# Replanning the first transfers of a fused linear-attention and LoRA-expert FFN kernel

## The chip, the cores and the metric

The kernel runs on one core of one Trainium2 chip. The metric is device time in microseconds of one execution; three executions of the kernel before are known, and one more was recorded by the profiler.

## The reference, cut to what matters

```python
xn = layernorm(x)                        # x: 2 x 1024 tokens of 512 floats
Q = elu(heads(xn @ wq.T + bq)) + 1       # 16 heads of 32
K = elu(heads(xn @ wk.T + bk)) + 1
V = heads(xn @ wv.T + bv)
KV = einsum('bhsd,bhse->bhde', K, V)
att = (Q @ KV) / (Q . sum_s K + 1e-8)
att = att @ wo.T + bo
# FFN of 1376 with a router over 8 experts (top 2), shared and expert LoRA of rank 8
gate = xn @ W_gate + lora(xn) + expert_lora(xn, w)
up   = xn @ W_up   + lora(xn) + expert_lora(xn, w)
ffn  = (silu(gate) * up) @ W_down + lora + expert_lora
return x + att + ffn
```

All is float32. Each operand of a product is split into a rounded part (`_h`, made by ACT, `round_to`) and a remainder (`_l`, made by DVE, `sub`), and PE computes each product as three matmuls: high by high, high by low, low by high (`product`, L1196 to L1198).

## The kernel before

The engines are programmed each by itself, with an order written out by hand and semaphores between them. ACT is ScalarE, DVE VectorE, POOL GpSimd, PE TensorE; SP is SyncE, which here only issues transfers. The kernel has three stages: stage 1 runs over 16 tiles of 128 tokens, the attention and the FFN over groups of four tiles. The change is all in stage 1 and its preparation.

*Preparation.* SP loads x tile 0, the identity, wk (`w_raw[:, 0]`, 1 MB), x tile 1, wv (`w_raw[:, 1]`, 1 MB) and `a_raw` (the LoRA and router columns) in this order. ACT rounds wk in quarters k = 0 to 3, then wv in quarters, then a; DVE forms the remainders in the same order (`wsetl_done` counts them). DVE's layer norm of tile 0 goes through POOL (`rstd_of`) and PE's `transpose_tokens(0)`. PE meanwhile runs filler matmuls of the identity (`keep_busy`, L1264), five before these transposes and four behind them, and then the first product of wk. POOL issues five small constants (`bk`, `ebias`, `earlier`, `bq`, `zmask`) after `rstd_of(0)`.

*Stage 1 for tile t* (`stage1` in each engine's part). PE: K of tile t (`ps_k`), transposes of tile t + 1 (L1213), in even tiles `keys_by_values` of the two tiles before (L1225), V (`ps_va`, `ps_vz`), then `lora_transposed(t - 2)` (L1234), which needs DVE's `zst`. ACT: first `tokens_hi(t + 1)`, which rounds the transposed tokens into `xt[:, slot]` (L660), slot being the parity of the tile. It waits until the store of that slot's former tile, t - 1, has landed:

```python
act.wait_ge(xt_ready, t + 1)
wait(act, scr_xd[s], 16 * uses)
round_to(xt_h[:, s].rearrange("p k n -> p (k n)"), ps_xt[:]).then_inc(xth_done, 1)
```

DVE: `kb`, the routing comparison, `tokens_lo(t + 1)` (L849), then `lora_weighted(t - 2)` (`zst`), statistics and normalisation of tile t + 2, `zraw`, and at the end `lora_lo(t - 2)` (L914), after which SP may store z of tile t - 2. Tiles 2 to 7 are a loop of pairs on ACT, DVE and PE; tiles 8 to 15 are written out (there ACT and DVE also split wq, at tiles 8 to 11, and wo, at 12 to 15).

*SP in stage 1.* For tile t it loads x of tile t + 3 (L391) and stores the split tokens to `scr_x` (L425). It then stores z of tile t - 2 (L415), in even tiles of the loop loads `x3a` back from `scr_x` (L405), and loads a chunk of `dn` (L442). All its transfers run on one queue. Its loop covers tiles 2 to 9 in four passes, tiles 10 to 15 are written out. In the loop it stores z of tile 2p behind the stage1 of tile 2p + 2. Behind the stage1 of tile 0 it issues eight constants of later stages (L431 to L433: `hmask`, `hcol`, `hrow_raw`, `lomask`, `bdn_raw` 512 KB, `sb_dn` 256 KB, `bv_b`, `bo_b`, a broadcast of one row of 2 KB to all 128 partitions), then the whole of wo and wq (L435, L436) into the two halves of `w_raw`, which are free once `wsetl_done` has reached 8.

## Time and profile before

| what | us |
|---|---|
| median of 3 runs (lowest, highest) | 675.92 (674.55, 676.27) |
| the profiled execution, its own time | 675.29 |
| its span | 673.5 |
| PE busy | 661.8 (98%) |
| DVE, ACT, POOL busy | 375.6, 256.3, 126.9 |

Times in the profile are microseconds from the start of the span. "Idle before <-releaser" is the engine's own wait and what ended it. A matmul's duration is modelled and overlaps the next; the distance between starts is the pace. `bank` stands for any PSUM bank. L660 and L849 are the helpers for rounding and remainder, so the name of the tile tells what is meant. The profile's granted clock reads 1.00 throughout; PE's two speeds in the first microseconds are seen only in the pitch of its products.

### The profile page before, as it was taken

To read this page: it belongs to the slowest core of one execution; us is meant where nothing else is said; L and a number is where in the kernel's file an instruction comes from. 1 tells how busy PE (TensorE), PEld (TensorE's weight loads), DVE (VectorE), ACT (ScalarE), POOL (GpSimd) and SP (SyncE) were. 2 spreads that over 40 slices of the span, in tenths; PEclk is the share of its full clock that TensorE was granted. 3 is DMA by queue.
4 is the path that set the end of the run, shared out by engine and by line. 5 is a ranking of instruction groups with operands and counts; after the bars stand their busy time and mean duration, and the time that the engine had idled before them with its cause. 6 is when DMAs were issued, how large, how long until landed. Compare 5 with 4: busy or idle time off the path is not lost.

```text
span 673.5 us, 10336 instructions
## 1 busy us (share of the span) xinstructions
PE 661.8 (98%) x3568; PEld 544.2 (81%) x3568; DVE 375.6 (56%) x696; ACT 256.3 (38%) x412; POOL 126.9 (19%) x290
## 2 busy tenths in 40 slices
PE   7999999999999999999999999999999999999998
PEld 6889899977677788888888888888888888888886
DVE  5577788778775966344346433445444336534433
ACT  4343445467235324323233332333233314323321
POOL 3456666635256130000000000000000000000000
PEclk9999999999999999999999999999999999999999
DMA  7946566753853679940024100012400002300001
GB/s 222 328 158 225 194 202 203 249 213 150 307 218 115 253 242 3 43 161 0 0 79 169 82 0 0 0 63 78 187 0 0 0 0 78 126 0 0 0 0 62
DMA packets 40634, 74.21 MB, mean 110 GB/s; under 512 B 19280, under 2 KB 19920, under 8 KB 38688
## 3 DMA queue, kind: packets, MB, share of 16 engines
q1 hardware_dynamic: 40400, 73.56, 37.5%
q0 software_dynamic: 208, 0.30, 0.4%
q8 instruction: 16, 0.26, 0.2%
q14 instruction: 10, 0.08, 0.0%
HBM read 52.81 MB, written 21.04 MB: 110 GB/s over the span
## 4 chain that ended last, share of the span: by engine, by line
PE 89%; DVE 4%; issue 2%; ACT 1%; POOL 1%; DMA 1%; SPq 0%; POOLq 0%; DVEq 0%; ACTq 0%
PE bank L1196 20%; PE bank L1197 19%; PE bank L1198 19%; PE bank L1438 18%; PE bank L1411 6%; PE bank L1424 2%; DVE den L1049 1%; PE bank L1422 1%; DMA w_raw<-in_wkT 1%; PE bank L1213 1%; PE bank L1225 1%; PE bank L1311 1%; DVE qf_odd L1007 1%; PE bank L1449 1%; PE bank L1451 1%
## 5 line engine op out<-in xcount | busy, mean ns | idle before, releaser
L1196 PE MATMUL bank<-x,up_h 128*128 128x512 f32 (+1 forms) x352 | 137.1, 390 | 0.2 <-DVE x3r L1014 0.2
L1197 PE MATMUL bank<-x,up_h 128*128 128x512 f32 (+1 forms) x352 | 137.2, 390 | 0.0
L1198 PE MATMUL bank<-x,up_l 128*128 128x512 f32 (+1 forms) x352 | 137.1, 390 | 0.0
L1139 DVE TENSOR_TENSOR hf<-bank,silu 128x512 f32<-128x512 f32 x44 | 30.4, 691 | 155.4 <-issue 135.6
L1438 PE MATMUL bank<-dn,hid_h 128*128 128x512 f32 x352 | 108.7, 390 | 0.0
L660 ACT ACTIVATE hid_h<-hf 128x512 fp32r<-128x512 f32 x44 | 27.8, 632 | 142.4 <-DVE hf L1139 142.4
L1196 PEld LDWEIGHTS bank<-x,up_h 128*128 128x128 f32 x352 | 66.1, 188 | 16.5 <-issue 0.7
L1438 PEld LDWEIGHTS bank<-dn,hid_h 128*128 128x128 f32 x352 | 65.9, 188 | 14.7 <-DVE res L1158 0.6
L1197 PEld LDWEIGHTS bank<-x,up_h 128*128 128x128 f32 x352 | 66.1, 188 | 14.2
L1198 PEld LDWEIGHTS bank<-x,up_l 128*128 128x128 f32 x352 | 66.1, 188 | 13.8
L849 DVE TENSOR_TENSOR up_l<-up_raw,up_h 128x1024 fp32r<-128x1024 f32 x44 | 55.0, 1249 | 26.9 <-ACT up_h L660 26.9
L1438 PE MATMUL bank<-dn,hid_l 128*128 128x512 f32 x176 | 68.5, 389 | 0.0
L660 ACT ACTIVATE up_h<-up_raw 128x1536 fp32r (+1 forms) x44 | 64.5, 1473 | 1.7 <-DVE qf_odd L1007 1.7
L809 ACT ACTIVATE silu<-bank 128x512 f32<-128x512 f32 x44 | 26.3, 599 | 101.0 <-PE bank L1411 101.0
L1411 PE MATMUL bank<-z,up_h 128*128 128x512 f32 x176 | 54.2, 389 | 0.0
L849 DVE TENSOR_TENSOR hid_l<-hf,hid_h 128x512 fp32r<-128x512 f32 x44 | 30.5, 692 | 35.5 <-ACT hid_h L660 35.5
L660 ACT ACTIVATE dn<-dn_raw 128x576 fp32r (+1 forms) x44 | 30.1, 683 | 33.5 <-PE bank L1424 22.6
L1196 PE MATMUL bank<-va_h,xt 128*128 128x384 f32 (+1 forms) x128 | 41.5, 324 | 0.0
L1197 PE MATMUL bank<-va_l,xt 128*128 128x384 f32 (+1 forms) x128 | 40.3, 315 | 0.0
L1198 PE MATMUL bank<-va_h,xt 128*128 128x384 f32 (+1 forms) x128 | 40.3, 315 | 0.0
L849 DVE TENSOR_TENSOR up_h<-up_raw,up_h 64x256 fp32r<-64x256 f32 x88 | 38.6, 439 | 0.6
L1438 PEld LDWEIGHTS bank<-dn,hid_l 128*128 128x128 f32 x176 | 33.0, 188 | 7.0
(165 smaller groups left out, 1081.7 us busy)
## 6 DMA issues: line engine op xcount, KB each, us to landing
x<-scr_x SPq DMA_DIRECT2D x7, 2048.0 KB, 9.3
up_raw<-in_ffn_up SPq DMA_DIRECT2D x11, 768.0 KB, 7.9
scr_x<-xt SPq DMA_DIRECT2D x16, 512.0 KB, 5.3
xin<-in_x SPq DMA_DIRECT2D x16, 256.0 KB, 4.6
scr_z<-zt SPq DMA_DIRECT2D x16, 256.0 KB, 2.0
x3r<-in_x SPq DMA_DIRECT2D x16, 256.0 KB, 3.5
scr_att<-x3r SPq DMA_DIRECT2D x16, 256.0 KB, 2.7
z<-scr_z SPq DMA_DIRECT2D x4, 1024.0 KB, 4.9
```

Of the source, the lines that this page charges most:

```text
L660: return nc.scalar.activation(dst, src, ACT.Copy)
L809: nc.scalar.activation(silu[:], ps_g[:], ACT.Silu).then_inc(silu_done, 1)
L849: return nc.vector.tensor_tensor(dst, a, b.bitcast(F32), ALU.subtract)
L1007: nc.vector.tensor_tensor(qf[g % 2][:, c, :], qf[g % 2][:, c, :], qexp[:, c % 2, :], ALU.add).then_inc(q_done, 1)
L1049: nc.vector.reciprocal(den[:], den[:]).then_inc(rden_done, 1)
L1139: nc.vector.tensor_tensor(hf[:], ps_u[:], silu[:], ALU.mult).then_inc(h_done, 1)
L1196: nc.tensor.matmul(dst, lh, rh, start=start, stop=False, **kw)
L1197: nc.tensor.matmul(dst, lh, rl, start=False, stop=False, **kw)
L1198: return nc.tensor.matmul(dst, ll, rh, start=False, stop=stop, **kw)
L1411: last = nc.tensor.matmul(dst[:], up_h[:, s, col:col + P], z4[:, :, a * 2 + b, :], start=False, stop=(b == 1))
L1424: return nc.tensor.matmul(ps_zd[0:ER, :], dn_h[:, s, DNB - 1], hid_l[:, s, :], start=False, stop=last, skip_group_check=True)
L1438: d = nc.tensor.matmul(ps_out[j][:], h[:, s, cols], w[:, s, 0:DNB - 1], start=(first and i == 0), stop=False, skip_group_check=True)
```

## The change

- wk is loaded in quarters with a semaphore each: 1 and 3 by SP, 0 and 2 by ACT (its own queue). wv is loaded in four quarters by SP. ACT rounds tile 0's tokens after quarter 1, not 0; DVE likewise forms their remainder after quarter 1. DVE takes the statistics of tile 1 after the first quarter of wv, and normalises it after the third.
- a is split in two halves on ACT and DVE; PE waits for the second at its k = 2 of the first tile (`upper`).
- POOL issues `bk` once wk's last quarter has landed, and the other four constants after `rstd_of(1)`. DVE waits for `bk` alone before the tiles, and for the other four behind `zraw` of tile 0, where it also makes `nbq`.
- SP issues one quarter of wq and one of wo at the head of each of its four loop passes. The eight constants go behind the z store of tile 8, in tile 10 (`load_constants`).
- ACT waits for `wq_in` and `wo_in` at the splits; ACT and DVE wait for `s2_in` where the constants are first read.

```diff
-STAGE2_LOADS = 10
+STAGE2_LOADS = 8
...
             load_x(0, 0)
             sp.dma_start(ident[:], dram["ident"]).then_inc(ident_in, 16)
-            sp.dma_start(w_raw[:, 0], dram["wkT"]).then_inc(wk_in, 16)
+            for k in range(1, KD, 2):
+                sp.dma_start(w_raw[:, 0, k], dram["wkT"][:, k]).then_inc(wk_in[k], 16)
             load_x(1, 1)
-            sp.dma_start(w_raw[:, 1], dram["wvT"]).then_inc(wv_in, 16)
+            for k in range(KD):
+                sp.dma_start(w_raw[:, 1, k], dram["wvT"][:, k]).then_inc(wv_in[k], 16)
...
             stage1(0, 0)
-            for dst, name in ((hmask, "headmask"), (hcol, "headcol"), (hrow_raw, "headrow"), (lomask, "lomask"), (bdn_raw, "b_dn"), (sb_dn, "sb_dn")):
-                sp.dma_start(dst[:], dram[name]).then_inc(s2_in, 16)
-            sp.dma_start(bv_b[:], dram["bv"]).then_inc(s2_in, 16)
-            sp.dma_start(bo_b[:], dram["bo"].to_broadcast([P, D])).then_inc(s2_in, 16)
+            stage1(1, 1)
+
+            def load_constants():
+                for dst, name in ((hmask, "headmask"), (hcol, "headcol"), (bv_b, "bv"), (hrow_raw, "headrow"),
+                                  (lomask, "lomask"), (bdn_raw, "b_dn"), (sb_dn, "sb_dn")):
+                    sp.dma_start(dst[:], dram[name]).then_inc(s2_in, 16)
+                sp.dma_start(bo_b[:], dram["bo"].to_broadcast([P, D])).then_inc(s2_in, 16)
+
             sp.wait_ge(wsetl_done, 2 * KD)
-            sp.dma_start(w_raw[:, 0], dram["woT"]).then_inc(s2_in, 16)
-            sp.dma_start(w_raw[:, 1], dram["wqT"]).then_inc(s2_in, 16)
...
-            stage1(1, 1)
-            with sp.Fori(0, GT) as p:
+            with sp.Fori(0, KD) as p:
+                sp.dma_start(w_raw[:, 1, bass.ds(p, 1)], dram["wqT"][:, bass.ds(p, 1)]).then_inc(wq_in, 16)
+                sp.dma_start(w_raw[:, 0, bass.ds(p, 1)], dram["woT"][:, bass.ds(p, 1)]).then_inc(wo_in, 16)
                 stage1(2 * p + 2, 0)
...
                 if t < TILES - 1:
                     store_z(t - 2)
+                if t == 2 * GT + 2:
+                    load_constants()
                 if t < FC:
                     load_dn(t - 2)
...
             rstd_of(0)
-
-            for dst, name in ((bk_b, "bk"), (eb_b, "ebias")):
-                pool.dma_start(dst[:], dram[name].to_broadcast([P, dst.shape[1]])).then_inc(consts_in, 16)
+            pool.wait_ge(wk_in[KD - 1], 16)
+            pool.dma_start(bk_b[:], dram["bk"].to_broadcast([P, D])).then_inc(bk_in, 16)
+            pool.wait_ge(wv_in[1], 16)
+            rstd_of(1)
+            pool.dma_start(eb_b[:], dram["ebias"].to_broadcast([P, E])).then_inc(consts_in, 16)
...
-            rstd_of(1)
             rstd_of(2)
...
+            act.wait_ge(vare_done, 1)
+            for k in range(0, KD, 2):
+                act.dma_start(w_raw[:, 0, k], dram["wkT"][:, k]).then_inc(wk_in[k], 16)
             act.sem_inc(scr_zd, 16)
-            act.wait_ge(wk_in, 16)
             for k in range(KD):
+                act.wait_ge(wk_in[k], 16)
                 round_to(wk_h[:, k], w_raw[:, 0, k]).then_inc(wseth_done, 1)
-                if k == 0:
+                if k == 1:
                     tokens_hi(0, 0, 0)
-            act.wait_ge(wv_in, 16)
             for k in range(KD):
+                act.wait_ge(wv_in[k], 16)
                 round_to(wv_h[:, k], w_raw[:, 1, k]).then_inc(wseth_done, 1)
             act.wait_ge(a_in, 16)
-            round_to(a_h, a_raw[:]).then_inc(wseth_done, 1)
+            for k in range(0, KD, 2):
+                round_to(a_h[:, k:k + 2], a_raw[:, k:k + 2]).then_inc(wseth_done, 1)
...
                 nc.vector.tensor_copy(zraw[:, s], ps_z).then_inc(zraw_done, 1)
+                if first:
+                    dve.wait_ge(consts_in, 64)
+                    nc.vector.tensor_scalar(nbq[:], bq_c[:], -1.0, None, ALU.mult).then_inc(nbq_done, 1)
...
-                if k == 0:
+                if k == 1:
                     tokens_lo(0, 0)
-            stats_of(1, 1, 0)
             for k in range(KD):
                 dve.wait_ge(wseth_done, KD + k + 1)
                 sub(wv_l[:, k], w_raw[:, 1, k], wv_h[:, k]).then_inc(wsetl_done, 1)
-                if k == 1:
+                if k == 0:
+                    stats_of(1, 1, 0)
+                if k == 2:
                     normalise(1, 1)
```

The order of SP's transfers around tiles 10 and 11, where the scr_x store that ACT waits for at tile 12 stands. Before:

```order
L391 DMA xin<-in_x 128x512
L425 DMA scr_x<-xt 128x1024
L415 DMA scr_z<-zt 128x512
L442 DMA dn_raw<-in_ffn_dn 128x576
L391 DMA xin<-in_x 128x512
L425 DMA scr_x<-xt 128x1024
```

The same place in the change (`bdn_raw` and `sb_dn_sb` are constants of the down projection):

```order
L394 DMA xin<-in_x 128x512
L430 DMA scr_x<-xt 128x1024
L420 DMA scr_z<-zt 128x512
L439 DMA hmask<-in_headmask 128x4
L439 DMA hcol<-in_headcol 128x128
L439 DMA bv_b<-in_bv 128x128
L439 DMA hrow_raw<-in_headrow 128x128
L439 DMA lomask_sb<-in_lomask 128x1
L439 DMA bdn_raw<-in_b_dn 128x1024
L439 DMA sb_dn_sb<-in_sb_dn 128x512
L440 DMA bo_b<-in_bo 128x512
L448 DMA dn_raw<-in_ffn_dn 128x576
```

The eight constants now stand between the z store of tile 8 and the load of `dn`, ahead of x of tile 14 and the scr_x store of tile 11.

DVE's queue before the first `kb` (tile 0), before the change:

```order
L849 TENSOR_TENSOR wk_l<-w_raw,wk_h 128x512
L849 TENSOR_TENSOR xt<-bank,xt 128x512
L849 TENSOR_TENSOR wk_l<-w_raw,wk_h 128x512 x3
L853 BN_STATS stats<-xin 128x6
L856 MEMSET spare 128x1
L857 BN_AGGR mv<-stats 128x2
L849 TENSOR_TENSOR va_l<-w_raw,va_h 128x512 x2
L862 TENSOR_SCALAR xn<-xin,mv,rstd 128x512
```

and in the change:

```order
L865 TENSOR_TENSOR wk_l<-w_raw,wk_h 128x512 x2
L865 TENSOR_TENSOR xt<-bank,xt 128x512
L865 TENSOR_TENSOR wk_l<-w_raw,wk_h 128x512 x2
L865 TENSOR_TENSOR va_l<-w_raw,va_h 128x512
L869 BN_STATS stats<-xin 128x6
L872 MEMSET spare 128x1
L873 BN_AGGR mv<-stats 128x2
L865 TENSOR_TENSOR va_l<-w_raw,va_h 128x512 x2
L878 TENSOR_SCALAR xn<-xin,mv,rstd 128x512
```

The remainder of tile 0's tokens (`xt`) moves behind the second quarter of wk; the statistics of tile 1 move behind the first quarter of wv.

## Rows read from the trace of the kernel before

**Rows 1.** The page, part 1: busy time, share of the span and instructions.

```profile
PE 661.8 (98%) x3568; PEld 544.2 (81%) x3568; DVE 375.6 (56%) x696; ACT 256.3 (38%) x412; POOL 126.9 (19%) x290
```

**Rows 2.** TensorE's waits over the whole run: total, times, longest (us).

```profile
PE bank L1234 <- DVE zst L904: 1.3, 1, 1.3
PE bank L1196 <- DVE xt L849: 1.2, 1, 1.2
```

**Rows 3.** Chain of waits, first 18 us: start us, us, what.

```profile
1.67 6.38 DMA w_raw<-in_wkT
...
10.09 0.79 PE bank L1196
10.89 0.43 PE bank L1197
...
13.69 0.23 PE bank L1198
```

**Rows 4.** Timeline, first 10 us: start us, us, engine, line, work, [idle before <-releaser].

```profile
3.77 2.50 PE L1264 MATMUL bank<-ident_sb 128*128 128x128 f32 x10 [3.77 <-DMA ident_sb<-in_ident]
...
7.01 1.91 PE L1264 MATMUL bank<-ident_sb 128*128 128x128 f32 x8
...
9.35 0.68 DVE L849 TENSOR_TENSOR xt<-bank,xt 128x512 fp32r<-128x512 f32 x1
```

**Rows 5.** Timeline of PE, 28 to 107 us: L1225 and L1234.

```profile
28.85 0.77 PE L1225 MATMUL bank<-vf,kf 128*32 128x33 f32 x64
...
34.80 0.44 PE L1234 MATMUL bank<-ident_sb,zst 128*128 128x128 f32 x2 [1.34 <-DVE zst L904]
...
46.26 0.77 PE L1225 MATMUL bank<-vf,kf 128*32 128x33 f32 x64
...
61.35 0.77 PE L1225 MATMUL bank<-vf,kf 128*32 128x33 f32 x64
...
72.90 0.38 PE L1234 MATMUL bank<-ident_sb,zst 128*128 128x128 f32 x2
...
106.59 0.78 PE L1225 MATMUL bank<-vf,kf 128*32 128x33 f32 x64
```

**Rows 6.** Timeline of ACT: the roundings of tokens.

```profile
33.06 0.60 ACT L660 ACTIVATE xt<-bank 128x512 fp32r<-128x512 f32 x1 [5.86 <-DMA scr_x<-xt]
...
63.06 0.60 ACT L660 ACTIVATE xt<-bank 128x512 fp32r<-128x512 f32 x1 [2.06 <-DMA scr_x<-xt]
...
69.53 0.60 ACT L660 ACTIVATE xt<-bank 128x512 fp32r<-128x512 f32 x1 [0.80 <-PE bank L1213]
```

**Rows 7.** Timeline of SP: DMA issues, start us, us of issuing.

```profile
15.46 0.43 SPq L431 DMA_DIRECT2D hmask<-in_headmask  x1
...
19.44 0.43 SPq L433 DMA_DIRECT2D bo_b<-in_bo  x1
...
21.57 0.46 SPq L425 DMA_DIRECT2D scr_x<-xt  x1
...
54.72 0.35 SPq L415 DMA_DIRECT2D scr_z<-zt  x1
...
62.13 0.35 SPq L415 DMA_DIRECT2D scr_z<-zt  x1
...
69.92 0.35 SPq L415 DMA_DIRECT2D scr_z<-zt  x1
...
99.77 0.34 SPq L415 DMA_DIRECT2D scr_z<-zt  x1
...
101.13 0.43 SPq L425 DMA_DIRECT2D scr_x<-xt  x1
```

**Rows 8.** DMA issues at 21.5 and 101.1 us: KB, us to landing.

```profile
scr_x<-xt SPq DMA_DIRECT2D x1, 512.0 KB, 11.5
...
scr_x<-xt SPq DMA_DIRECT2D x1, 512.0 KB, 4.7
```

**Rows 9.** DMA issues of the first 45 us: KB, us to landing.

```profile
bo_b<-in_bo SPq DMA_DIRECT2D x1, 256.0 KB, 6.0
```

More of the change, by code:

```diff
@@ L249, in program @@
         consts_in = sem("consts_in")
+        bk_in = sem("bk_in")
         ident_in = sem("ident_in")
-        wk_in = sem("wk_in")
-        wv_in = sem("wv_in")
+        wk_in = [sem(f"wk_in{k}") for k in range(KD)]
+        wv_in = [sem(f"wv_in{k}") for k in range(KD)]
         a_in = sem("a_in")
@@ L292, in program @@
         s2_in = sem("s2_in")
+        wq_in = sem("wq_in")
+        wo_in = sem("wo_in")
         nbq_done = sem("nbq_done")
@@ L685, in stage1 @@
                 if isinstance(t, int) and t in WQ_PART:
-                    act.wait_ge(s2_in, 16 * STAGE2_LOADS)
+                    act.wait_ge(wq_in, 16 * KD)
                     round_to(wq_h[:, WQ_PART[t]], w_raw[:, 1, WQ_PART[t]]).then_inc(wqh_done, 1)
                 if isinstance(t, int) and t in WO_PART:
+                    act.wait_ge(wo_in, 16 * KD)
                     round_to(wo_h[:, WO_PART[t]], w_raw[:, 0, WO_PART[t]]).then_inc(woh_done, 1)
@@ L768, in _ @@
             act.wait_ge(kf_done, TILES)
+            act.wait_ge(s2_in, 16 * STAGE2_LOADS)
             round_to(hrow[:], hrow_raw[:]).then_inc(hrow_done, 1)
@@ L969, in _ @@
                 sub(wv_l[:, k], w_raw[:, 1, k], wv_h[:, k]).then_inc(wsetl_done, 1)
-                if k == 1:
+                if k == 0:
+                    stats_of(1, 1, 0)
+                if k == 2:
                     normalise(1, 1)
-            dve.wait_ge(wseth_done, 2 * KD + 1)
-            sub(a_l, a_raw[:], a_h).then_inc(wsetl_done, 1)
+            for k in range(0, KD, 2):
+                dve.wait_ge(wseth_done, 2 * KD + k // 2 + 1)
+                sub(a_l[:, k:k + 2], a_raw[:, k:k + 2], a_h[:, k:k + 2]).then_inc(wsetl_done, 1)
             dve.sem_inc(kvacc_done, 1)
-            dve.wait_ge(consts_in, 80)
+            dve.wait_ge(bk_in, 16)
             def heads_of(b):
+                dve.wait_ge(s2_in, 16 * STAGE2_LOADS)
                 for c in range(KD):
@@ L984, in heads_of @@
                                         hmask[:].unsqueeze(1).unsqueeze(3).to_broadcast([P, KD, HC, DK]), ALU.mult).then_inc(kvm_done, 1)
-            nc.vector.tensor_scalar(nbq[:], bq_c[:], -1.0, None, ALU.mult).then_inc(nbq_done, 1)
             tiles(dve, stage1)
@@ L1198, in product, with tile_of @@
                 return nc.tensor.matmul(dst, ll, rh, start=False, stop=stop, **kw)
-            def tile_of(dst, s, wh, wl, split_before=None):
+            def tile_of(dst, s, wh, wl, split_before=None, upper=None):
                 for k in range(KD):
@@ L1204, in tile_of @@
                         pe.wait_ge(wsetl_done, split_before + k + 1)
+                    if upper is not None and k == 2:
+                        pe.wait_ge(wsetl_done, upper)
                     last = product(dst, (xt_h[:, s, k, :], xt_l[:, s, k, :]), (wh[:, k, :], wl[:, k, :]),
@@ L1254, in stage1 @@
                     pe.wait_ge(wsetl_done, 2 * KD + 1)
-                tile_of(ps_vz, s, va_h[:, :, VA:], va_l[:, :, VA:]).then_inc(vz_ready, 1)
+                tile_of(ps_vz, s, va_h[:, :, VA:], va_l[:, :, VA:], upper=2 * KD + 2 if first else None
+                        ).then_inc(vz_ready, 1)
                 if behind(t, 2):
```

## Prediction

> **What bounds the kernel now.** I read the page first, then TensorE's waits, then the chain of waits and the timelines at the places the change touches. TensorE (PE) is busy 661.8 us of the span [rows 1]: nothing counts but what stops it or slows its matmuls. The list of its waits [rows 2] holds two that this change can reach. One is 1.2 us before the first product. The other is 1.3 us before the transposes of L1234, near 34 us.
>
> The start: the chain of waits [rows 3] runs through the load of wkT (1 MB, landed at 8.05), its first rounding on ACT, the first remainders on DVE, and reaches PE at 10.09. PE had run filler matmuls of L1264 and four transposes from 3.77 up to 8.92 (7.01 + 1.91) [rows 4]. From 10.89 the products of L1196 to L1198 come every 0.43 us, from 13.69 on every 0.23 us [rows 3]. The first pitch belongs to the 1.2 GHz level of PE's clock, the second to 2.4 GHz. The clock rose about 3.3 us after the products had begun.
>
> The stall near 34: PE's `keys_by_values` (L1225) starts once per pair of tiles; from 46.26 to 61.35 is 15.09 us, an undisturbed pair. From 28.85 to 46.26 is 17.41 [rows 5], so the disturbed pair lost 2.3 us. ACT rounded the tokens of tile 3 at 33.06 after 5.86 us of waiting for a store of scr_x [rows 6]. That store (tile 1's, slot 1) was issued at 21.57 [rows 7] and landed 11.5 us later [rows 8]. Ahead of it in the SP queue were eight constants, all of wo and wq and an x tile.
>
> **The change part by part.**
>
> *Start.* wk comes in quarters, so ACT's first two roundings need 512 KB, not 1 MB. Before, the 1 MB (behind x tile 0 and ident) took 6.4 us from its issue [rows 3]; half of it I estimate to be there 1.5 to 2.5 us sooner, by 5.6 to 6.6. Two roundings, each of the tokens' size (0.60) [rows 6], end by 7.9 at the latest, then the tokens' own rounding (0.60) and remainder (0.68) [rows 4] by 9.2. PE is held by its own filler until 8.92 anyway. So the first product moves from 10.09 to about 9.0: **-1.1 us**. The bounds are 0 (quarters no faster than the whole) and -2.0. The second is reached if the clock also rises sooner: eight products ran at the slow pitch [rows 3], and the 0.2 us they lose each cannot all be had, since DVE's remainders of wv and a (8 operations of about 0.68 and two small ones between 9.0 and 15) then hold PE. The splits of a in halves, the later POOL constants (eb, earlier, bq, zmask) and the negation of bq moved behind tile 0 I cost at nothing. What covers them is that PE needs what follows on DVE, tile 2's tokens, only some 5 us later. If the POOL constants land late, up to 1 us of DVE waiting hides there.
>
> *The stall near 34.* Constants, wo and wq no longer lie ahead of tile 1's store; only one quarter of each is issued, behind it. **-2.3 us** [rows 5]. What is late next is the ordinary pair time, so the whole of it comes back.
>
> *wq and wo by quarters.* Each of four loop passes issues two more transfers (512 KB) on SP, ahead of the even tile's x load and store. The odd tile's store already has a 512 KB transfer (x3a) ahead of it, and it shows what that does. From the store of z at 54.72 [rows 7] to ACT's tokens at 63.06 [rows 6], which waited for the landing, is 8.34 us. PE did not stall in that pair [rows 5]. By this pattern the even tile's tokens come at 62.13 + 8.34 + some 0.3 of issue = 70.8 in place of 69.53 [rows 6, 7]. From tokens to L1234 took 1.74 us (33.06 to 34.80) [rows 5, 6], so 72.5, and PE reaches L1234 at 72.90 [rows 5]: 0.4 us of slack. The lag feeds back, as the next z store hangs on these tokens. I take **+0.2 us**; bounds 0 and +2.6 (a rival, below).
>
> *The constants at tile 10.* They do not vanish, they move into SP's queue between the z store of tile 8 (99.77) and the scr_x store of tile 11 (101.13) [rows 7]. ACT's rounding of tile 13's tokens waits for that store, exactly as tile 3's waited for tile 1's. Before, the burst took from 15.46 to the end of bo's issue at 19.87, 4.4 us [rows 7], so the store is issued at 105.5. Bounds for its landing T. Lowest: only the issue is late and it lands 4.7 us on [rows 8], or less if an issue costs 0.43 throughout: 109.4 to 110.3. Highest: bo landed 6.0 us after 19.44 [rows 9], at 25.4, so 10.0 us after the burst began. In the new place that is 110.1, with dn, x and the store (1.06 MB) behind it. The 2.75 MB behind bo before (wo, wq, x, scr_x) took from 25.4 to 33.07, 360 GB/s, so 2.9 us more: 113.0. I take 112.0, nearest to the upper end, because the same eight transfers and the same broadcast are in front of the same store. The loss: before, tokens at 33.06 were 4.21 us behind L1225 at 28.85 and cost 2.33 us [rows 5, 6]. Here L1225 is at 106.59 [rows 5]. The loss is 2.33 + (T - 106.59 - 4.21) = T - 108.5: **+3.5 us**, bounds +0.9 and +4.5.
>
> The Trainium skill ("DMA: Bandwidth & Descriptors", Specifications) puts the fabric's ceiling at 435 GB/s. By it alone the 2.08 MB from bdn to the store, issued from about 102.9, would be in by some 109.7 (an estimate with its 2 us of fixed cost), and this term would be +1.2. The rows speak against it: bo, 256 KB, took 6.0 us to land [rows 9], where a store of twice its size took 4.7 [rows 8].
>
> *Their readers.* ACT's, DVE's and POOL's new waits on s2_in come at tile 14 and later, 25 us behind the loads: nothing. The same holds for wq_in at tile 8, where ACT needs the last quarter several us after its issue.
>
> **The sum.** -1.1 - 2.3 + 0.2 + 3.5 = +0.3 us, against the profiled execution's own 675.29 us (its span is 673.5). That is 675.6. The profiled run lies 0.6 us under the median of the three, 675.92; they spread over 1.7 us, more than most single terms here. About 0.3% (2.0 us) is what a measurement of this kernel can tell from no change: below 673.9 counts as faster, above 677.9 as slower.
>
> **Rivals.**
>
> 1. *The burst at tile 10 is cheap* (the lower bound: T near 109.4 to 110.3, +0.9 to +1.8). For it: in the new place no 2 MB of weights follows. Against it: the same broadcast. It gives 675.29 - 1.1 - 2.3 + 0.2 + 0.9 to 1.8 = 673.0 to 673.9. Chance 0.22.
> 2. *The clock rises sooner.* Closing the 1.2 us gap leaves PE busy from the first filler on. For it: the clock rose 3.3 us after the products began, and with no gap the filler may count too. Against it: 5 us of filler and transposes did not raise it before. It takes 0.9 us more off: 674.7, or 672.1 to 673.0 with rival 1. Chance 0.10, half of that below 673.9. The Trainium skill ("TensorE: Matmul & The Clock Gate", Part 4) says transposes do not count as busy for the clock; the four transposes lie between the two batches of filler, and the trace agrees so far as the clock stayed low across them.
> 3. *The stores become the loop's bound*: slower. Place: SP's queue at the head of each pass. The landing of the even tile's store is followed 6.9 us later by the next odd z store (63.06 to 69.92 for the other parity [rows 6, 7]), which starts the next store. With 8.34 us from z to landing that loop takes 15.2 us against PE's 15.09, so it would be level, with the slack above to spare. From about 0.4 us of added landing time on it decides. If the 512 KB add 1.3 us, three passes lose 1.3 each, less some 1.3 of slack: +2.6 in place of +0.2, 678.0. Chance 0.10.
> 4. *The start does not do what it says*: the quarters, in 2 KB rows, land as late as the whole did. Then 675.29 - 2.3 + 0.2 + 3.5 = 676.7. Chance 0.08. The Trainium skill ("DMA: Bandwidth & Descriptors", Issuing engines are not separate DMA queues) says that a second issuing engine saves only issue time.
>
> The forecast itself has 0.50, from 673.8 to 677.2. Faster: 0.22 + 0.05 + 0.05 of the forecast's edge = 0.32. Slower: 0.10. Same: 0.58. The range, 672.4 to 677.7, leaves out rival 3 and the lowest corner of rivals 1 and 2.
>
> **What would show it.** The first product at 8.9 to 9.3, the clock's rise at 12.3 to 13.4. No wait of ACT for scr_x near 33, and 15.1 us from the first L1225 to the second. A wait of ACT for scr_x of 4 us or more at tile 12, with PE idle before L1234 some 111 us into the old time scale. Even-tile tokens waiting on scr_x in the loop. I am wrong if that pair stays at 15.1 us, or if the pairs of the loop grow.

## The result, and the profile after

| | before | the change |
|---|---|---|
| median of 5 runs (lowest, highest), us | 674.94 (674.55, 676.27) | 679.88 (678.98, 681.89) |
| ratio (95% interval) | | 1.0073 (1.0060 to 1.0086) |
| profiled execution, its own time; span | 675.29; 673.5 | 679.69; 677.9 |
| PE busy | 661.8 | 662.6 |

The change is 4.9 us slower, outside the range of 672.4 to 677.7. PE does the same work in the same time; the loss is in its waits. TensorE's waits in the profile after (total, times, longest, in us), the three that the change touched:

```profile
PE bank L1257 <- DVE zst L920: 5.0, 2, 3.2
...
PE bank L1217 <- DVE va_l L865: 0.8, 1, 0.8
PE bank L1217 <- DVE xt L865: 0.6, 1, 0.6
```

The wait of 1.2 us at the start became 0.6 and 0.8. The one of 1.3 us for `zst` [rows 2] became two, 5.0 us together. (Lines have shifted: L1225 is now L1248, L1234 is L1257, L1196 to L1198 are L1217 to L1219, L1213 is L1236.) PE's timeline after, `keys_by_values` once per pair of tiles, and each stop behind the start:

```profile
28.16 0.77 PE L1248 MATMUL bank<-vf,kf 128*32 128x33 f32 x64
43.26 0.77 PE L1248 MATMUL bank<-vf,kf 128*32 128x33 f32 x64
58.57 0.77 PE L1248 MATMUL bank<-vf,kf 128*32 128x33 f32 x64
74.02 0.77 PE L1248 MATMUL bank<-vf,kf 128*32 128x33 f32 x64
87.47 0.44 PE L1257 MATMUL bank<-ident_sb,zst 128*128 128x128 f32 x2 [1.75 <-DVE zst L920]
91.06 0.77 PE L1248 MATMUL bank<-vf,kf 128*32 128x33 f32 x64
106.14 0.77 PE L1248 MATMUL bank<-vf,kf 128*32 128x33 f32 x64
113.98 0.44 PE L1257 MATMUL bank<-ident_sb,zst 128*128 128x128 f32 x2 [3.24 <-DVE zst L920]
126.24 0.77 PE L1248 MATMUL bank<-vf,kf 128*32 128x33 f32 x64
140.88 0.77 PE L1248 MATMUL bank<-vf,kf 128*32 128x33 f32 x64
```

The starts of the same line before that [rows 5] does not hold, from PE's timeline of the kernel before:

```profile
76.43 0.77 PE L1225 MATMUL bank<-vf,kf 128*32 128x33 f32 x64
...
121.70 0.77 PE L1225 MATMUL bank<-vf,kf 128*32 128x33 f32 x64
...
136.35 0.76 PE L1225 MATMUL bank<-vf,kf 128*32 128x33 f32 x64
```

Subtracting start from start gives the whole account, in us:

| stretch | before | after | difference |
|---|---|---|---|
| up to the first start | 28.85 | 28.16 | -0.7 |
| first pair (the stall near 34) | 17.41 | 15.10 | -2.3 |
| two pairs of the loop | 30.17 | 30.76 | +0.6 |
| pair with tiles 8 and 9 | 15.08 | 17.04 | +2.0 |
| pair with tiles 10 and 11 | 15.08 | 15.08 | 0 |
| pair with tiles 12 and 13 (the stop behind the burst) | 15.11 | 20.10 | +5.0 |
| next pair | 14.65 | 14.64 | 0 |
| sum | | | +4.5 (spans: +4.4) |

**The start.** PE's timeline after, first products of wk, the wait in V of tile 0, K of tile 1:

```profile
9.48 0.51 PE L1217 MATMUL bank<-wk_h,xt 128*128 128x512 f32 x1 [0.61 <-DVE xt L865]
9.82 0.39 PE L1218 MATMUL bank<-wk_l,xt 128*128 128x512 f32 x1
10.06 0.39 PE L1219 MATMUL bank<-wk_h,xt 128*128 128x512 f32 x1
...
15.20 0.44 PE L1217 MATMUL bank<-va_h,xt 128*128 128x384 f32 x1 [0.82 <-DVE va_l L865]
...
17.84 0.50 PE L1217 MATMUL bank<-wk_h,xt 128*128 128x512 f32 x1
```

Products come every 0.23 us from 9.82 on, the pitch of 2.4 GHz that the kernel before reached near 13.4 [rows 3]. So the clock rose about 3.5 us sooner, yet K of tile 1 starts only 0.7 us sooner (17.84 against 18.57): V of tile 0 has to wait for DVE's remainders. PE was no longer what bound this stretch. These are single executions, and the sooner rise is not shown to come from the change: a run with the old start ("The kernel before, its whole block one store later", below) has the fast pitch from its second product too.

**Tile 8 and the burst.** ACT's timeline after: tokens of an even tile in the loop, the first rounding of wq (tile 8), the tokens of tile 10, the tokens of tile 13:

```profile
68.54 0.60 ACT L670 ACTIVATE xt<-bank 128x512 fp32r<-128x512 f32 x1 [2.71 <-DMA scr_x<-xt]
...
82.50 0.63 ACT L670 ACTIVATE wq_h<-w_raw 128x512 fp32r<-128x512 f32 x1 [4.25 <-DMA w_raw<-in_wqT]
...
85.17 0.60 ACT L670 ACTIVATE xt<-bank 128x512 fp32r<-128x512 f32 x1 [1.25 <-DMA scr_x<-xt]
...
112.25 0.60 ACT L670 ACTIVATE xt<-bank 128x512 fp32r<-128x512 f32 x1 [5.91 <-DMA scr_x<-xt]
```

DVE's remainder of that quarter of wq:

```profile
83.24 0.69 DVE L865 TENSOR_TENSOR wq_l<-w_raw,wq_h 128x512 fp32r<-128x512 f32 x1 [2.23 <-ACT wq_h L670]
```

The issues of SP's queue that these wait for (the last quarter of wq, the first and last constant, the scr_x store of tile 11):

```profile
77.48 0.36 SPq L451 DMA_DIRECT2D w_raw<-in_wqT  x1
...
100.31 0.43 SPq L439 DMA_DIRECT2D hmask<-in_headmask  x1
...
103.65 0.43 SPq L440 DMA_DIRECT2D bo_b<-in_bo  x1
...
105.08 0.43 SPq L430 DMA_DIRECT2D scr_x<-xt  x1
```

ACT at tile 8 waits until all four quarters of wq are there, and the fourth is issued only in the pass that brings tile 8's own store. The wait reaches PE through DVE, which stands 2.23 us for the rounding and then has a full queue up to `zst`. A second wait ends at nearly the same time: the tokens of tile 10 came at 85.17, released by the landing of tile 8's scr_x store. PE's stop (87.47, in tile 9) has both behind it; it is called the stop at tile 8 below. At tile 12 the store is issued 4.0 us later than before (105.08, not 101.13) and lands 7.1 us on, not 4.7 [rows 7, 8].

**The clock behind the long stop.** Windows of the profile after: stretch, then length, busy time of PE, PEld, DVE, ACT, POOL, then PEclk, DMA share, GB/s:

```profile
110.70:113.98 3.28, 0.04 (x1) 0.00 (x1) 1.11 (x5) 1.70 (x4) 0.00 (x0) 1.00 1.04 399
...
115.30:118.70 3.40, 3.40 (x10) 2.54 (x9) 2.60 (x7) 0.90 (x4) 2.76 (x9) 0.50 0.05 19
```

Shortly behind the idle time of 3.24 us the granted clock is 0.50 (1.2 GHz) for 3.4 us. By these figures, 3.4 us at half speed, the fall cost some 1.7 us (an estimate). The first window shows also that the 16 DMA engines were full (share 1.04, 399 GB/s) while PE stood.

### The profile page after: what moved, and what is told of

Read it like the earlier page. It is cut to its first block, busy times and chain, and to the rows that moved or that the text cites. A ratio compares the mean times of both kernels' runs of the same rounds, so it can differ in the third digit from the quotient of the medians.

```text
span 677.9 us, 10370 instructions
## 1 busy us (share of the span) xinstructions
PE 662.6 (98%) x3568; PEld 544.0 (80%) x3568; DVE 375.9 (55%) x697; ACT 256.4 (38%) x413; POOL 126.7 (19%) x290
## 4 chain that ended last, share of the span: by engine, by line
PE 78%; POOL 6%; issue 5%; DVE 5%; DMA 3%; ACT 2%; SPq 1%; POOLq 1%; ACTq 0%; DVEq 0%
PE bank L1462 17%; PE bank L1217 16%; PE bank L1218 16%; PE bank L1219 16%; PE bank L1435 6%; PE bank L1448 2%; DVE den L1070 1%; PE bank L1446 1%; DMA scr_x<-xt 1%; DMA w_raw<-in_wkT 1%; POOL vare L580 1%; POOL rstd L582 1%; DMA w_raw<-in_wqT 1%; POOL gt L607 1%; PE bank L1335 1%
## 5 line engine op out<-in xcount | busy, mean ns | idle before, releaser
L1217 PE MATMUL bank<-x,up_h 128*128 128x512 f32 (+1 forms) x352 | 137.1, 390 | 0.2 <-DVE x3r L1035 0.2
L1219 PE MATMUL bank<-x,up_l 128*128 128x512 f32 (+1 forms) x352 | 137.1, 389 | 0.0
L1217 PEld LDWEIGHTS bank<-x,up_h 128*128 128x128 f32 x352 | 66.1, 188 | 16.5 <-issue 0.7
L1219 PEld LDWEIGHTS bank<-x,up_l 128*128 128x128 f32 x352 | 66.1, 188 | 13.8
L1217 PE MATMUL bank<-va_h,xt 128*128 128x384 f32 (+1 forms) x128 | 41.9, 327 | 0.8 <-DVE va_l L865 0.8
L1219 PE MATMUL bank<-va_h,xt 128*128 128x384 f32 (+1 forms) x128 | 40.3, 315 | 0.0
```

The source lines that it names most:

```text
L1217: nc.tensor.matmul(dst, lh, rh, start=start, stop=False, **kw)
L1219: return nc.tensor.matmul(dst, ll, rh, start=False, stop=stop, **kw)
```

## The experiments

All line numbers within one kernel differ by one or two from those above where its edit adds or removes lines. Each batch is set against its own runs of the kernel before: 674.72 in the first (four kernels), 675.22 in the second (four), 674.84 in the third (four).

### ACT waits for each quarter alone

```diff
-                    act.wait_ge(wq_in, 16 * KD)
+                    act.wait_ge(wq_in, 16 * (WQ_PART[t] + 1))
```

> The change, with ACT waiting at tiles 8 to 11 for one more quarter of wq each time, not for all four at tile 8. Theory 1 (each loss has its own place: 2.0 us by ACT's wait of 4.25 us for wq at tile 8, 5.0 at tiles 12 and 13 by the burst of constants, 0.6 in the loop): the wait for wq is gone, the pair that took 17.0 us takes about 15.3, and the kernel is 1.7 to 2.0 us faster than the change (about 678). Theory 2 (the loop's stores have become the bound, and the stop at tile 8 is only where their lag comes due): ACT's tokens stay late, PE stops at the same place for scr_x, and under 0.7 us is gained.

Measured: 679.38 us, 1.0074 (1.0059 to 1.0089). PE's timeline, the stops at tile 8 and tile 12:

```profile
86.18 0.44 PE L1257 MATMUL bank<-ident_sb,zst 128*128 128x128 f32 x2 [0.94 <-DVE zst L920]
...
113.54 0.69 PE L1257 MATMUL bank<-ident_sb,zst 128*128 128x128 f32 x2 [4.07 <-DVE zst L920]
```

ACT's timeline, the tokens of tile 10:

```profile
84.44 0.60 ACT L670 ACTIVATE xt<-bank 128x512 fp32r<-128x512 f32 x1 [3.41 <-DMA scr_x<-xt]
```

The stop at tile 8 is halved, and PE reaches the pair of tile 12 1.3 us sooner (104.86, not 106.14). Then it stands 0.8 us longer, and in the profiles 0.5 us is left (spans of 677.4 and 677.9). In time it is not resolved: the ratios to the kernel before are 1.0074 here and 1.0073 in the change. The burst was issued 1.5 us sooner (98.81) too, but ACT's tokens came at 111.81, 0.4 us sooner. Here the gain ahead of a stop that transfers end was mostly lost in it. Why this store took longer behind its own issue (8.2 us from 103.60 to the tokens, against 7.2) no row settles. 0.9 us of stop is left at tile 8 and it is not wq's: the even tile's tokens (84.44) waited 3.41 us for a scr_x store there. The wait for wq is gone as theory 1 had it, but the gain is that of theory 2.

### Constants back to the beginning, the rest as in the change

```diff
             stage1(0, 0)
-            stage1(1, 1)
-
             def load_constants():
...
+            load_constants()
+            stage1(1, 1)
...
-                if t == 2 * GT + 2:
-                    load_constants()
```

> The change, with the eight constants back behind the store of tile 0; wq and wo stay by quarters in the loop. Theory 1: the stop of 3.2 us at tile 12 and the slow matmuls behind it go (pair 15.1 in place of 20.1), and near 34 us nothing comes back, since constants alone leave tile 1's store landing near 27: 5 us faster than the change, about 675. Theory 2 (the burst only pays once wherever it stands): some 2.3 us come back near 34, and the gain is about 2.7.

Measured: 674.23 us, 0.9989 (0.9980 to 0.9998), 5.7 us under the change, as theory 1 had it. This one edit takes the whole loss back. The pair of tile 12 is 15.1 us again, and the first pair stays at 15.1: at the beginning the constants cost nothing once the 2 MB of wo and wq no longer follow. (Its profiled execution, 677.19, is the slowest of its 12: the stop at tile 8 was 2.21 us there, and the clock fell behind it.)

### The kernel before, its whole block one store later

The eight constants, wo and wq are issued behind `stage1(1, 1)` instead of ahead of it.

```diff
-            for dst, name in ((hmask, "headmask"), (hcol, "headcol"), ...
-            sp.dma_start(w_raw[:, 1], dram["wqT"]).then_inc(s2_in, 16)
...
             stage1(1, 1)
+            for dst, name in ((hmask, "headmask"), (hcol, "headcol"), ...
+            sp.dma_start(w_raw[:, 1], dram["wqT"]).then_inc(s2_in, 16)
             with sp.Fori(0, GT) as p:
```

> The kernel before, with the block of eight constants, wo and wq issued behind tile 1's store of scr_x, not ahead of it; nothing else. Theory 1 (what stops PE near 34 us is only that tile 1's store stands behind the block): ACT's wait of 5.9 us for scr_x goes, the pair of 17.4 us falls to 15.1 to 15.6 (tile 2's store, now behind the block, lands near 35, when it is just wanted), 1.8 to 2.3 us faster than before. Theory 2 (the bytes must be paid wherever they stand): the wait moves to tile 4's tokens and 0 to 0.5 us is gained.

Measured: 675.19 us, 1.0017 (1.0000 to 1.0033). PE's timeline:

```profile
9.27 0.50 PE L1195 MATMUL bank<-wk_h,xt 128*128 128x512 f32 x1 [1.32 <-DVE xt L848]
9.61 0.39 PE L1196 MATMUL bank<-wk_l,xt 128*128 128x512 f32 x1
...
28.25 0.77 PE L1224 MATMUL bank<-vf,kf 128*32 128x33 f32 x64
...
41.47 0.44 PE L1233 MATMUL bank<-ident_sb,zst 128*128 128x128 f32 x2 [1.51 <-DVE zst L903]
```

The stall near 34 is gone and stands at 41.5, on the next store of scr_x, with 1.51 us (1.34 before [rows 5]). 3.2 MB in one block has to be paid somewhere (theory 2): to move it is worth nothing, to spread it is (the runs with quarters, below). The first lines show something else. The start here is the old one, yet the first product comes at 9.27, the products behind it at 0.23 us each, and the first `keys_by_values` at 28.25, 0.6 us sooner than in the profile before and 0.1 later than in the change. With the new start that line stood at 26.98 to 30.42 in the profiled executions. So one pair of profiles does not price the start.

### The start alone

wk and wv in quarters as in the change, constants and the whole of wo and wq as before.

```diff
             stage1(0, 0)
-            stage1(1, 1)
...
+            load_constants()
+
             sp.wait_ge(wsetl_done, 2 * KD)
+            sp.dma_start(w_raw[:, 0], dram["woT"]).then_inc(wo_in, 16)
+            sp.dma_start(w_raw[:, 1], dram["wqT"]).then_inc(wq_in, 16)
+            stage1(1, 1)
...
             with sp.Fori(0, KD) as p:
-                sp.dma_start(w_raw[:, 1, bass.ds(p, 1)], dram["wqT"][:, bass.ds(p, 1)]).then_inc(wq_in, 16)
-                sp.dma_start(w_raw[:, 0, bass.ds(p, 1)], dram["woT"][:, bass.ds(p, 1)]).then_inc(wo_in, 16)
```

> The start of the change alone (quarters of wk and wv on two queues, a in halves, POOL's constants later), with the constants and the whole of wo and wq where the kernel before had them. Theory 1: first product near 9.5, K of tile 1 some 0.7 us sooner than before, the stall near 34 as before, and no stops at tiles 8 and 12: 0.7 us faster than before, up to 2 in a run where the clock rises sooner. Theory 2 (the start gives nothing in the runs' mean, as the clock's rise differs from run to run): within 0.3 us of before.

Measured: 675.48 us, 1.0006 (0.9997 to 1.0016). PE's timeline, and the window behind the stop (columns as above):

```profile
27.54 0.77 PE L1248 MATMUL bank<-vf,kf 128*32 128x33 f32 x64
...
34.82 0.44 PE L1257 MATMUL bank<-ident_sb,zst 128*128 128x128 f32 x2 [2.67 <-DVE zst L920]
```

```profile
36.00:39.20 3.20, 3.20 (x9) 2.46 (x9) 1.64 (x6) 0.90 (x4) 2.56 (x9) 0.50 0.00 0
```

PE arrives 1.3 us sooner than before (27.54, not 28.85) and goes on at the same moment, 34.82 against 34.80 [rows 5]: the store's landing sets it. The stop is 1.3 us longer, and behind it the clock fell, as it did not behind the shorter one. That holds for this execution: in eight of the twelve the mean granted clock was 1.000, in four 0.997, which is one such fall. While the stall stands, the start's gain is nothing (675.48 against 674.72).

### All three mended

Constants early, a wait per quarter, and the quarters of each pass behind the even tile's store.

```diff
...
             with sp.Fori(0, KD) as p:
+                stage1(2 * p + 2, 0)
                 sp.dma_start(w_raw[:, 1, bass.ds(p, 1)], dram["wqT"][:, bass.ds(p, 1)]).then_inc(wq_in, 16)
                 sp.dma_start(w_raw[:, 0, bass.ds(p, 1)], dram["woT"][:, bass.ds(p, 1)]).then_inc(wo_in, 16)
-                stage1(2 * p + 2, 0)
...
-                    act.wait_ge(wq_in, 16 * KD)
+                    act.wait_ge(wq_in, 16 * (WQ_PART[t] + 1))
```

> The change with three mends: the constants back behind tile 0's store, ACT waiting for one quarter of wq at a time, and the loop's quarters of wq and wo issued behind the even tile's store of scr_x, not ahead of it. Theory 1 (the extra bytes ahead of the stores that ACT waits for are the cause of all three stops, and there is idle time of the queue behind the even store): no stop before L1257 anywhere, all pairs at 15.1 us, no fall of the clock; 671.5 to 672.5, some 2.5 us faster than before and 7 to 8 faster than the change. Theory 2 (the store chain needs more than PE's 15.1 us per pair as soon as wq and wo are in the loop): pairs of 15.3 to 15.5 and a stop near tile 8 stay, 674 or more.

Measured: 671.94 us, 0.9952 (0.9940 to 0.9963): 3.3 us faster than the kernel before, some 8 us faster than the change. PE's timeline:

```profile
8.54 0.75 PE L1216 MATMUL bank<-wk_h,xt 128*128 128x512 f32 x1
...
26.98 0.77 PE L1247 MATMUL bank<-vf,kf 128*32 128x33 f32 x64
...
117.47 0.77 PE L1247 MATMUL bank<-vf,kf 128*32 128x33 f32 x64
```

Six pairs in 90.49 us, 15.08 each, and no wait for `zst`. The waits that share one semaphore are sound only because each quarter lands (some 5 us) long before the next is issued (15 us): the Trainium skill ("DMA: Bandwidth & Descriptors", Why a DMA increments its semaphore by 16 and not by 1) warns that with two transfers in flight on one semaphore the count can pass before the first is there. A semaphore for each quarter would be the form to keep.

### Is it bo's broadcast?

Only `bo` goes back to the beginning, seven constants stay at tile 10.

```diff
             stage1(0, 0)
+            sp.dma_start(bo_b[:], dram["bo"].to_broadcast([P, D])).then_inc(s2_in, 16)
             stage1(1, 1)
...
-                sp.dma_start(bo_b[:], dram["bo"].to_broadcast([P, D])).then_inc(s2_in, 16)
```

> The change, with one of the eight constants, the broadcast bo (256 KB), back behind tile 0's store; seven constants (0.96 MB) stay in tile 10. Theory 1 (bo's broadcast is the slow part of the burst, 2 to 2.5 us of it): tile 11's store lands 2.5 to 3 us sooner, PE's stop falls from 3.2 to about 0.7 us and the clock does not fall; 4 us faster than the change, about 676. Theory 2 (a byte is a byte; bo is a fifth of the burst): the stop falls by 0.5 (issue) to 1.1 us, to over 2 us; the clock still falls or not, 679 to 677.5.

Measured: 678.02 us, 1.0047 (1.0032 to 1.0062), 1.9 us under the change. PE's timeline:

```profile
112.91 0.44 PE L1257 MATMUL bank<-ident_sb,zst 128*128 128x128 f32 x2 [2.41 <-DVE zst L920]
```

The stop is 0.8 us shorter, ACT's tokens come at 111.17, 1.1 us sooner. An issue (0.48 us) and 256 KB at the 400 GB/s of the stretch (0.66 us) are 1.1 us. So bo weighs what its issue and its bytes weigh (theory 2); the other seven carry the rest. In this profile the clock did not fall, and the pair took 18.03 us (105.87 to 123.90), 2.1 less than in the change. But in four of the six executions the mean granted clock was 0.997, as in the change, so the clock is not shown to be the remainder of the 1.9 us, and no run here tells what is.

### The burst behind the store that is next

In tile 10 the constants go ahead of `store_z(8)`, directly behind the tile's own scr_x store, where SP's queue would be idle.

```diff
                 stage1(t, t % 2, more=(t + 3 < TILES))
+                if t == 2 * GT + 2:
+                    load_constants()
                 if t < TILES - 1:
                     store_z(t - 2)
-                if t == 2 * GT + 2:
-                    load_constants()
```

> The change, with the same burst of eight constants in tile 10, but issued behind tile 10's store of scr_x and ahead of the z store of tile 8 (SP waits there some 5 us for z with an empty queue). Theory 1 (what costs is that the burst delays tile 11's store): the burst is issued and mostly landed before z comes, tile 11's store lands near its old time or up to 1 us later, the stop at tile 12 goes; 4.5 to 5 us faster than the change, about 675. Theory 2 (the bytes must be paid in any place of that tile): the stop stays above 2 us.

Measured: 675.37 us, 0.9998 (0.9986 to 1.0009), 4.5 us under the change. PE's timeline:

```profile
111.25 0.44 PE L1257 MATMUL bank<-ident_sb,zst 128*128 128x128 f32 x2 [0.54 <-DVE zst L920]
```

SP's timeline, the first constant:

```profile
96.03 0.43 SPq L439 DMA_DIRECT2D hmask<-in_headmask  x1
```

The same bytes, in the same tile, two statements up in the code: of the 3.24 us of stop 0.54 are left, since the burst now starts at 96.03, some 4 us sooner, and the queue has gone through most of it when the next store comes. What cost the change its 5 us was the place in the queue, not the transfers.

### How much of it is the clock

Filler matmuls of the identity ahead of tile 12's `lora_transposed` keep PE at work through the stop: 24 in one kernel, 14 in the other.

```diff
+                if isinstance(t, int) and t == 12:
+                    keep_busy(ps_t, FILL)
                 if behind(t, 2):
                     lora_transposed(t - 2)
```

> The change, with 24 filler matmuls of the identity (as keep_busy has them) on PE at tile 12, ahead of L1257, in the 3.2 us in which PE stood idle; the results of the filler are used by nothing. It measures what the fall of the clock costs. Theory 1 (the idle time let the clock fall to 1.2 GHz for 3.4 us, from 115.3 to 118.7): the stop stays, the clock does not fall, tile 13's pace is undisturbed: 1.3 to 1.6 us faster than the change. Theory 2 (the slow stretch behind the stop has another cause): no gain, or 0.3 us lost where the filler is longer than the stop.

> e8 with 14 filler matmuls in place of 24. The 24 took 5.4 us, 2.0 us more than the stop, and still the next L1249 came only 0.3 us later than in the change: with the clock kept up, 1.6 us were won and 2.0 lost. Fourteen take 3.1 us and fit into the stop. Theory 1 (the fall of the clock costs 1.6 us): 1.3 to 1.7 us faster than the change, 678.2 to 678.6. Theory 2 (the clock's fall is worth nothing, the filler's end is hidden otherwise): as slow as the change, 679.9.

Measured: 679.96 us, 1.0076 (1.0055 to 1.0096) with 24, and 679.33 us, 1.0062 (1.0044 to 1.0079) with 14. PE's timelines, first with 24, then with 14:

```profile
110.55 5.52 PE L1291 MATMUL bank<-ident_sb 128*128 128x128 f32 x48
115.90 0.38 PE L1258 MATMUL bank<-ident_sb,zst 128*128 128x128 f32 x2
...
126.52 0.77 PE L1249 MATMUL bank<-vf,kf 128*32 128x33 f32 x64
```

```profile
110.21 3.29 PE L1291 MATMUL bank<-ident_sb 128*128 128x128 f32 x28
113.42 0.44 PE L1258 MATMUL bank<-ident_sb,zst 128*128 128x128 f32 x2
...
124.42 0.77 PE L1249 MATMUL bank<-vf,kf 128*32 128x33 f32 x64
```

In neither profile did the clock fall behind the filler. From the transposes to the next `keys_by_values` took 10.62 us with 24 and 11.00 with 14, against 12.26 in the change (113.98 to 126.24): the fall cost that stretch 1.3 to 1.6 us. 24 were too many: they ended 1.7 us behind the time that `zst` needs (tokens at 112.46, and 1.73 us from tokens to transposes, as in the change). The 14 ended just in time (111.69 and 113.42). With 14 the pair took 18.66 us, 1.4 less than the change, but the medians differ by 0.5 us only, in different batches, and their intervals overlap. With 14 the clock stayed up in every execution: the mean granted clock was 0.999 or 1.000 in all six, and 0.994 or 0.997 in all five of the change. The kernel before hints at a price in time: its executions at 0.997 had medians 1.1, 0.5 and 1.5 us above those at 1.000 in the three batches, which goes along with a fall but does not prove it the cause. So the clock's part is shown in the profiles, in the time it is not resolved.

### The kernel before with quarters in the loop

The old start, constants at the old place, quarters behind the even tile's store, with a wait for each quarter of wq.

```diff
-            sp.dma_start(w_raw[:, 0], dram["woT"]).then_inc(s2_in, 16)
-            sp.dma_start(w_raw[:, 1], dram["wqT"]).then_inc(s2_in, 16)
...
                 stage1(2 * p + 2, 0)
+                sp.dma_start(w_raw[:, 1, bass.ds(p, 1)], dram["wqT"][:, bass.ds(p, 1)]).then_inc(wq_in, 16)
+                sp.dma_start(w_raw[:, 0, bass.ds(p, 1)], dram["woT"][:, bass.ds(p, 1)]).then_inc(wo_in, 16)
```

> The kernel before with only the transfers of wq and wo changed: by quarters in the loop behind the even store (as in e5), the constants where they were, the start as it was. Beside e5 (671.9) it prices the start where no stall near 34 stands in its way. Theory 1 (e4 gained nothing from the start because the stall near 34 ends at a time set by the transfers, and ate it): this kernel is 2.3 us faster than before, 672.9, and e5 is 1.0 us faster than it. Theory 2 (the start gives nothing anywhere): as fast as e5 within 0.4 us, and 3.3 us faster than before.

Measured: 672.90 us, 0.9973 (0.9962 to 0.9984): 1.9 us under the kernel before, all pairs 15.1 us, no wait for `zst`. The stall's removal alone is worth this. The mended kernel with the new start lies 1.0 us below it (671.94; by the ratios, since the batches differ, 1.4, with intervals that just touch): that is what the start is worth when no stall takes it back.

### The two mends of the loop, each taken away

The mended kernel with the quarters at the head of the pass again, as in the change:

```diff
             with sp.Fori(0, KD) as p:
-                stage1(2 * p + 2, 0)
                 sp.dma_start(w_raw[:, 1, bass.ds(p, 1)], dram["wqT"][:, bass.ds(p, 1)]).then_inc(wq_in, 16)
                 sp.dma_start(w_raw[:, 0, bass.ds(p, 1)], dram["woT"][:, bass.ds(p, 1)]).then_inc(wo_in, 16)
+                stage1(2 * p + 2, 0)
```

> e5 with the loop's quarters of wq and wo again at the head of each pass, ahead of the even store; constants early and one-quarter waits stay. It prices the place of the quarters alone. Theory 1 (the even store is delayed by their 512 KB; the lag feeds back through z): pairs of 15.1 to 15.4 and a stop of about 0.9 us at tile 8 as in e1; 1 to 1.5 us slower than e5. Theory 2 (the place does not matter once the waits for all quarters are gone): within 0.3 us of e5.

Measured: 674.07 us, 0.9976 (0.9964 to 0.9988). And the mended kernel with the wait for all four quarters:

```diff
-                    act.wait_ge(wq_in, 16 * (WQ_PART[t] + 1))
+                    act.wait_ge(wq_in, 16 * KD)
```

> e5 with ACT's wait at tile 8 for all four quarters of wq again, the quarters behind the even store. The last quarter is then issued about 1.7 us later than in the change. Theory 1 (that wait stops ACT, and through it the tokens): ACT waits 5 us or more for wq, PE stops 2 to 3 us at tile 8; 2.5 to 4 us slower than e5. Theory 2 (it is the lag of the stores, not the wait): 0 to 1 us slower than e5.

Measured: 673.47 us, 0.9974 (0.9963 to 0.9984). PE's timelines, the stop at tile 8 in the first and in the second, then ACT's in the second:

```profile
89.16 0.44 PE L1256 MATMUL bank<-ident_sb,zst 128*128 128x128 f32 x2 [1.77 <-DVE zst L919]
```

```profile
86.06 0.44 PE L1256 MATMUL bank<-ident_sb,zst 128*128 128x128 f32 x2 [1.32 <-DVE zst L919]
```

```profile
81.09 0.63 ACT L669 ACTIVATE wq_h<-w_raw 128x512 fp32r<-128x512 f32 x1 [4.46 <-DMA w_raw<-in_wqT]
```

Each alone brings back a stop at tile 8 and 1.5 to 2.1 us by the medians (by the ratios, since the batches differ, 1.6 for the place of the quarters and 1.5 for the wait). The kernel that lacks both mends (constants early, above) is 2.3 us above the mended one, 2.5 by the ratios, less than the two prices together. They are two causes of one stop, so their prices do not add. To mend one of the two gains 0.2 to 1.0 us (from medians to ratios), to mend both gains 2.3 to 2.5.

## Why the prediction was wrong

**The frame held.** PE's work did not change, its waits and clock made the whole difference, and the pairs of `keys_by_values` accounted for all of it. What failed is the sum of the terms.

**The start, -1.1: measured -0.7.** The first product came at 9.48, not 9.0: ACT's part ended at 8.50 as reckoned, but DVE had two remainders of wk in front of the tokens':

```profile
7.53 1.29 DVE L865 TENSOR_TENSOR wk_l<-w_raw,wk_h 128x512 fp32r<-128x512 f32 x2 [1.53 <-ACT wk_h L670]
8.74 0.68 DVE L865 TENSOR_TENSOR xt<-bank,xt 128x512 fp32r<-128x512 f32 x1
```

The prediction's sum left these two out (the lines are from DVE's timeline after). Rival 2's clock did rise sooner, and bought little for the reason given there: DVE's remainders held PE (the wait of 0.82 us at 15.20). But the sooner rise came in a run with the old start as well, and the -0.7 lies within what the first `keys_by_values` varies by from one profiled execution to the next, so it is luck as much as a measure. In time, with no stall behind it, the start is worth 1.0 to 1.4 us, as forecast. The prediction did not see that such a gain is lost when a stop that transfers end comes behind it; the start alone measured nothing.

**The stall near 34, -2.3: right.** 17.41 became 15.10.

**wq and wo by quarters, +0.2: measured +0.6 in the loop, and a share of the stop at tile 8.** The mechanism was as told: from the z store (59.54) to the even tile's tokens (68.54) took 9.0 us, where the prediction had 8.34 + 0.3, and 0.4 us of slack were all there was. Over the profiled executions with quarters ahead of the store those two pairs took 30.2 to 30.8 us in place of 30.17, so they lost up to 0.6 us. The rest of the lag came due at tile 8: in the mended kernel with the quarters ahead again, and a wait for each quarter alone, the two pairs lost nothing and the pair of tile 8 took 17.07 us, 2.0 more, with a stop of 1.77. In time the place of the quarters costs 1.6 to 2.1 us. This was rival 3's mechanism, at 0.6 to 0.8 of its price of 2.6; the term of 0.2 was too small by 1.4 to 1.9.

**"Their readers: nothing" was the other step that failed: the rest of the +2.0 at tile 8.** The prediction had ACT need the last quarter several us behind its issue. It did not read the wait's number: at tile 8 ACT needs one quarter but waits for four, and the fourth, issued at 77.48, landed 5 us later. The rounding came at 82.50 after 4.25 us, DVE's remainder behind it, and so `zst` was late. With the quarters behind the store and only this wait wrong, the stop is 1.32 us and the kernel 1.5 us slower. The lag of the stores stood at the same place, so to mend this wait alone let PE pass tile 8 1.3 us sooner in the profile and gave nothing that the time resolves (1.0074 against 1.0073).

**The constants at tile 10, +3.5: measured +5.0.** T was right: 112.25, where the prediction said 112.0. The burst put the store's issue 4.0 us later, not 4.4. Of the 1.5 us missing, 0.25 is T, and 0.45 is PE, which arrived sooner (106.14, not 106.59) at a stop whose end does not move. The last 0.8 lies behind the stop: the pair lost 1.8 us more than its stop of 3.24, where the prediction's scale (2.3 us lost on a stop of 1.3) had 1.0. The runs with filler put the clock's fall at 1.3 to 1.6 us of these 1.8. The prediction carried the loss behind a short stop over to a long one, and across that length the clock level changed. "The same broadcast" as the reason for T fell: bo weighs its bytes. So that T came out near 112.0 is in part luck.

**The rivals.** The cheap burst did not occur. For the slower side the prediction had one rival, the stores in the loop. Its lag was one of the two causes of the stop at tile 8, the wait for all quarters was in no rival, and the burst's upper bound, 4.5 us, had no room for the clock. With +2.0 and +5.0 in place of 0 and +3.5 the sum is +3.8; with the loop and the start as measured it is +4.6, the account up to rounding.

**The steps that failed** are thus three: the quarters' term (+0.2; alone it measured 1.6 to 2.1), the readers' term (0; alone it measured 1.5, the two together 2.3 to 2.5), and the loss at tile 12 (+3.5; it measured 5.0, the clock's fall behind the long stop being what the sum did not have).

**What the cause is,** by the runs: beside PE's 15.1 us per pair there is a second bound, nearly level with it, the circle z store, scr_x store, landing, ACT's tokens, DVE's `zst`, next z store (the circle is read from the order of the queues; what the rows show is that a scr_x store's landing ends the stops near 34, at 41.5 and at tile 12, and one of the two waits at tile 8). What SP's one queue issued ahead of a scr_x store lengthened it, and the same burst issued where the queue had time to spare cost next to nothing. The change took 3.2 MB out from ahead of one such store, put 1.2 MB ahead of another, and half a MB ahead of each even tile's in the loop.

## What to carry to other kernels

In a queue like SP's here, a transfer's place relative to the store that an engine waits for decides its price: put loads that nobody needs soon directly behind that store, in small pieces, not ahead of it. Check each wait's number against the issue time of the last transfer it counts, not against the first. Here a gain ahead of a stop that a transfer ends was worth nothing until the stop was gone, so the stop comes first. Price a term by the kernels' times with and without it: one profile each cannot tell 0.7 us at the start from the spread.

## What the runs showed of the hardware

- PE's clock fell to the lower level for about 3.4 us after idle times of 2.21, 2.67, 3.24 and 4.07 us, and after one of only 1.90 us ahead of the first product (the kernel before with quarters in the loop: 8.04 to 9.94, granted clock 0.50 from 10.5 to 13.5). It did not after 2.41 us (bo early), 2.07 us (24 filler matmuls) and 1.90 us (14 filler matmuls, both at tile 8). So between 1.9 and 2.4 us the stop's length alone does not decide. The Trainium skill ("TensorE: Matmul & The Clock Gate", Why this matters for your kernels) names idle gaps between bursts as what drops the clock; the trace agrees that they do. A fall is worth 1.3 to 1.7 us here.
- The clock's first rise is not fixed by the instructions: with the old start products ran at 0.23 us from 13.7 on in the kernel before and from the second product, 9.6, in the run with its block one store later. With the new start it was 9.8 in the change, 9.12 in the mended kernel, where PE had no gap at all behind the filler, and only from about 16 on in the mended kernel with the quarters ahead, whose profiled execution (676.75) is the slowest of its twelve.
- A full DMA system moved 399 to 406 GB/s (share 1.02 to 1.05), but with bo's broadcast in flight 202 GB/s at a share of 0.90 (106 to 109 us of the change); without it (bo early, the same window) 321 GB/s at 1.00. Yet to take bo out shortened the wait by no more than its issue and bytes. These two do not quite fit, and no run here tells why.
